# Moving the maxima and turns of Wk, Wv and Wo between the first batch's projections in an attention kernel on one Trainium2 core

## The reference

```python
def ref(x, adj, Wq, Wk, Wv, Wo):            # x: 32,256,512  adj: 32,256,256  W*: 512,512
    h = jnp.maximum(_layernorm(x, axis=-1), 0.0)
    q, k, v = (split_heads(h @ W.T) for W in (Wq, Wk, Wv))     # 16 heads of 32
    a = jnp.einsum('bhnd,bhmd->bhnm', q, k) * D ** (-0.5) + 2 * adj[:, None]
    row_nonzero = jnp.any(a != 0, axis=-1, keepdims=True)
    p = softmax(where(row_nonzero, a, -inf)); p = where(isnan(p), 0, p)
    o = jnp.einsum('bhnm,bhmd->bhnd', p, v)
    return x + merge_heads(o) @ Wo.T
```

## Time and profile before

| what | value |
|---|---|
| median of 3 runs | 1030.49 us (1030.35 to 1031.45) |
| profiled execution, its own time | 1030.06 us |
| its span, first to last instruction | 1028.3 us |
| mean granted PE clock | 0.983 of full speed |
| busy: PE, DVE, ACT, POOL | 980.3, 880.8, 930.1, 886.2 us |
| first exponentials on ACT | at 46.71 us |

### The profile page before, as it was taken

One profiled execution on the slowest core, in us unless ns is written; L12 is line 12 of the kernel. 1 busy time (PEld: TensorE's weight loads), 2 busy tenths in 40 slices (PEclk: granted clock), 3 DMA queues, 4 the chain that ended last, 5 costly groups with the idle time before them and its releaser, 6 DMA issues.

```text
span 1028.3 us, 34209 instructions
## 1 busy us (share of the span) xinstructions
PE 980.3 (95%) x11596; PEld 662.6 (64%) x11596; DVE 880.8 (86%) x3218; ACT 930.1 (90%) x3025; POOL 886.2 (86%) x1064
## 2 busy tenths in 40 slices
PE   6779999999999999999999999999999999999976
PEld 5556666666666666676666666666666666666733
DVE  6788998888899888899888889988888998888873
ACT  3499999999999999999999999999999999999992
POOL 1189998999999999999999999999999999999894
PEclk9899999999999999999999999999999999999978
DMA  6089999999999899999999999999999998999995
GB/s 245 11 144 173 190 185 170 191 181 187 187 188 194 174 187 175 190 186 189 188 176 185 182 186 183 192 172 189 179 186 190 187 196 173 187 175 167 164 173 128
DMA packets 569582, 182.62 MB, mean 178 GB/s; under 512 B 542784, under 2 KB 550976, under 8 KB 569408
## 3 DMA queue, kind: packets, MB, share of 16 engines
q1 hardware_dynamic: 569408, 180.43, 93.8%
HBM read 29.36 MB, written 16.78 MB: 45 GB/s over the span
## 4 chain that ended last, share of the span: by engine, by line
PE 40%; POOL 31%; ACT 19%; issue 6%; DVE 2%; DMA 1%; ACTq 0%; SPq 0%; POOLq 0%; DVEq 0%
PE ps L953 26%; POOL p L394 17%; ACT probs L488 13%; PE ps L1025 5%; PE ps L971 5%; POOL xn L374 4%; POOL o_lo L416 4%; ACT p L501 4%; POOL o_hi L413 2%; POOL rstd L368 2%; PE ps L836 2%; ACT v_hi L528 2%; POOL norm L403 2%; DVE w_max L589 1%; PE ps L999 1%
## 5 line engine op out<-in xcount | busy, mean ns | idle before, releaser
L394 POOL TENSOR_TENSOR p<-probs,p 128x512 f16<-128x512 f32 x512 | 588.7, 1160 | 86.9 <-ACT p L501 82.7
L488 ACT ACTIVATE probs<-logits,row_min 128x256 f32<-128x256 f32 x1024 | 508.7, 502 | 2.6 <-DVE row_min L669 2.6
L669 DVE CUSTOM_DVE_ANT_0 logits<-ps,adj_s,sigma 128x256 f32<-128x256 f32 x1024 | 441.3, 476 | 20.2 <-PE ps L971 13.2
L501 ACT ACTIVATE p<-probs 128x512 f16<-128x512 f32 x512 | 318.6, 622 | 0.0
L953 PE MATMUL ps<-ht_hi,w_hi 128*128 128x256 f16 x1024 | 279.7, 273 | 1.2 <-DVE q_lo L731 1.2
L953 PE MATMUL ps<-ht_hi,w_lo 128*128 128x256 f16 x1024 | 279.3, 273 | 0.0
L953 PE MATMUL ps<-ht_lo,w_hi 128*128 128x256 f16 x1024 | 279.3, 273 | 0.0
L488 ACT ACTIVATION_READ_ACCUMULATOR probs<-logits,row_min 128x1 f32 x1024 | 200.2, 196 | 0.0
L953 PEld LDWEIGHTS ps<-ht_hi,w_hi 128*128 128x128 f16 x1024 | 100.2, 98 | 21.7 <-issue 6.8
L953 PEld LDWEIGHTS ps<-ht_lo,w_hi 128*128 128x128 f16 x1024 | 100.3, 98 | 14.6
L953 PEld LDWEIGHTS ps<-ht_hi,w_lo 128*128 128x128 f16 x1024 | 100.3, 98 | 11.7
(11 more groups left out here) (84 smaller groups left out, 1659.1 us busy)
## 6 DMA issues: line engine op xcount, KB each, us to landing
xs<-in_x SPq DMA_DIRECT2D x32, 512.0 KB, 4.5
out<-xs SPq DMA_DIRECT2D x64, 256.0 KB, 2.6
adj_raw<-in_adj SPq DMA_DIRECT2D x32, 256.0 KB, 4.0
pt<-p SPq DMA_TRANSPOSE x512, 3.4
w_nat<-in_L_gnn_Wq SPq DMA_DIRECT2D x1, 1024.0 KB, 6.4
w_nat<-in_L_gnn_Wk SPq DMA_DIRECT2D x1, 1024.0 KB, 9.1
w_nat<-in_L_gnn_Wv SPq DMA_DIRECT2D x1, 1024.0 KB, 11.3
w_nat<-in_L_gnn_Wo SPq DMA_DIRECT2D x1, 1024.0 KB, 13.2
```

Source lines behind the costliest of these rows:

```text
L394: g.tensor_tensor(p16[:, c % 2, k, 1], probs[:, h % 4].rearrange("p u n -> p (u n)"), p16[:, c % 2, k, 0], ALU.subtract).then_inc(p_split, 1)
L488: e = a.activation(probs[:, h % 4, u, :], logits[:, h % 4, u, :], ACT.Exp, bias=row_min[:, t.par(d), u, h:h + 1], scale=-1.0, accum_out=ro ...
L501: a.activation(p16[:, c % 2, k, 0], probs[:, h % 4].rearrange("p u n -> p (u n)"), ACT.Copy)\
L669: v.tensor_tensor_reduce(out=logits[:, h % 4, u, :], in0=ps[:, S_BANK + h % HC, N * u:N * u + N], in1=adj_s[:, t.par(d), u, :], scale=sigm ...
```

## The change

The change adds no arithmetic and takes none away. It does four things in the first batch.

- Wk's whole chain leaves the prologue. Its maximum, row maximum, scale and low parts go to steps 0 to 3 on DVE, its high parts to step 3 on ACT; on PE `turn_max(1)` comes behind the 24 products of the first half of Q, `spread_max(1)` and `turn_weights(1)` behind the next 12.
- Wv's chain goes a step or so later: maximum still in step 4, row maximum 6 to 7, scale 7 to 8, and on PE the turn of the maximum 7 to 8 (so behind all of K's second half) and the rest from 8 to 9. Wo's maximum goes from step 4 to step 10 on DVE, its turn of the maximum from 10 to 11, its spread from 11 to 12.
- The first projection on each weight waits for the chunk that it multiplies with next, not for all four.
- POOL's wait for two scales moves from the slot's head to just before `adj_s`.

```diff
@@ pool @@
             def scale_adj(t):
                 pool.wait_ge(adj_in[t.par(1)], 16 * t.half(1) + 16)
+                if t.first:
+
+                    pool.wait_ge(scales_ready, 2)
...
             def slot(t):
-                if t.first:
-
-                    pool.wait_ge(scales_ready, 2)
@@ scalar @@
             take_h(first, 1, 1, 2)
-            take_weights(1)
...
-                    if t.first and s == 8:
-                        take_weights(2)
+                    if t.first and s in (3, 9):
+                        take_weights(1 + s // 9)
@@ vector @@
             take_h(first, 1, 0, 1)
-            weight_max(1)
-            weight_row_max(1)
             weight_rest(0)
             take_h(first, 1, 1, 2)
-            weight_scale(1)
-            weight_rest(1)
...
-                        if s in (3, 4):
-                            weight_max(s - 1)
-                        if s in (6, 10):
-                            weight_row_max(2 + s // 10)
-                        if s in (7, 11):
-                            weight_scale(2 + s // 11)
-                        if s == 8:
-                            weight_rest(2)
+                        if s in (0, 4, 10):
+                            weight_max({0: 1, 4: 2, 10: 3}[s])
+                        if s in (1, 7, 11):
+                            weight_row_max({1: 1, 7: 2, 11: 3}[s])
+                        if s in (2, 8, 12):
+                            weight_scale({2: 1, 8: 2, 12: 3}[s])
+                        if s in (3, 8):
+                            weight_rest({3: 1, 8: 2}[s])
@@ tensor @@
             turn_h(first, 1, 1)
-            turn_max(1)
-            spread_max(1)
-            turn_weights(1)
...
-                    if t.first and j in (0, 2, 6):
-
-                        pe.wait_ge(wt_taken, NC * (1 + {0: 0, 2: 1, 6: 2}[j]))
...
-                for o, l, r, start, stop in products[half * part:half * part + half]:
+                for i in range(half * part, half * part + half):
+                    o, l, r, start, stop = products[i]
+                    if t.first and j in (0, 2, 6) and i < 12 and i % 3 == 0:
+
+                        pe.wait_ge(wt_taken, NC * {0: 0, 2: 1, 6: 2}[j] + i // 3 + 1)
...
-                        if s in (7, 10):
-                            turn_max(2 + s // 10)
                         if s in (8, 11):
-                            spread_max(2 + s // 11)
-                        if s == 8:
+                            turn_max(2 + s // 11)
+                        if s in (9, 12):
+                            spread_max(2 + s // 12)
+                        if s == 9:
                             turn_weights(2)
...
                     project(t, s)
+                    if t.first and s == 1:
+                        turn_max(1)
+                    if t.first and s == 2:
+                        spread_max(1)
+                        turn_weights(1)
```

## The result

The changed kernel takes 1034.11 us, the median of 7 runs (1033.17 to 1035.79), against 1030.35 us of the kernel before beside it (7 runs, 1029.26 to 1031.45). The ratio is 1.0042, 95% interval 1.0031 to 1.0054. The prediction was 1034.0, range 1031.9 to 1036.0, slower. The profiled execution took 1034.11 us with a span of 1032.3, 4.0 more than before.

The account below looks back on a forecast made before the run. DVE's work and waits up to Wo's row maximum were taken to set the end. Waits of 6.45 us against 2.93 gave +3.5, end times +3.75, taken as +3.6: 1033.7 profiled, median 1034.0, range 1031.9 to 1036.0.

Parts of the forecast that it names:

- What bounds it: First batch: DVE's work and waits ahead of Wo's row maximum set the end; a shift there shifts everything behind it.
- that stretch at 1.8 us: Second slot's V products at the low clock, 71.8 to 74 us; without it some 1.8 us would be gone in either kernel.
- Q at 16.6: PE's first product of Q was to start at 16.6 us instead of 19.89, 3.3 us earlier.
- The waits of 2.5 and 1.2: DVE waits 2.5 us for PE's turn of Wk's maximum behind 24 products, 1.2 more for its spread behind 12.
- The fall of the clock: PE's granted clock was to be 0.50 from 17.3 to 20.7 us over Q, making 16 products slow.
- Forecast waits 0.65, 0.5, 0.8, 0.5: DVE's waits for Wv's turn (0.65), Wv's spread (0.5), ACT's first high part of Wv (0.8) and Wo's turn (0.5).
- The second `q_lo`: DVE's second low part of Q, behind Wv's maximum, was to come about 0.5 us later than 28.74.
- my two sums: DVE's delay up to Wo's row maximum: +3.5 us by summed waits, +3.75 by end times; +3.6 taken.
- C: Rival: the start of Q sets the first scores after all, 3.3 us earlier, 1027.2 us; chance 0.06.
- D: Rival: the shift is absorbed because later waits are fixed by something that doesn't shift, 1030.5 us; chance 0.07.
- B: Rival: same order effect, but PE's clock stays high over Q, 1032.3 us; chance 0.2.
- E: Rival: PE's clock stays low for longer, 1035.5 to 1036.3 us; chance 0.07.

Follow-up runs that it names:

- filler_before_scores: Kernel before plus 30 turns of Wq on PE, output unread, in the pause ahead of Wo's spread; 1027.64 us, ratio 0.9965.
- best: wo_behind_scores with Wv's turn and spread earlier, Wo's row maximum in step 13, its spread in 15, and 24 filler turns on PE; 1025.79 us, ratio 0.9954.
- turn_12_earlier: Changed kernel with PE's turn of Wk's maximum behind 12 products instead of 24, its spread behind 24 instead of 36; 1032.18 us, ratio 1.0027.
- clock_filler: Changed kernel plus 16 turns of Wq on PE, output unread, between the input's last turn and Q's first product; 1032.30 us, ratio 1.0027.
- wo_max_in_gap: Changed kernel with Wo's maximum on DVE directly behind Wk's, in the 2.47 us wait for PE; 1029.94 us, ratio 0.9999.
- late_only: Changed kernel with Wk's whole chain back in the prologue, only Wv's and Wo's parts at the later steps; 1030.37 us, ratio 1.0007.
- wo_behind_scores: Kernel before with all of Wo's chain moved behind the first scores (maximum in step 12); 1026.16 us, ratio 0.9972.
- chunk_waits_only: Kernel before with only the single-chunk waits and POOL's moved wait; 1030.02 us, ratio 0.9999.
- wk_only: Changed kernel with Wv's and Wo's chains at the steps of the kernel before, so only Wk's chain is moved; 1032.75 us, ratio 1.0033.

## Why the prediction was right

**What bounds it.** That DVE's work and waits up to Wo's row maximum set the start, and that this passes to the end nearly unchanged, held. In eleven of the thirteen kernels of the table it was 980.5 to 982.2 us from the first exponentials to the end of the span, while the exponentials' own start ranged from 43.33 to 50.99. In filler_before_scores and best it was 978.9 and 979.1. Both profiles are the fastest executions of their kernels, and in both the second slot's V products had the high pitch, 0.22, where the earlier trace rows has the low clock. But four other profiles had that as well, with 980.5 to 981.4 us, so what made the rest stays open. The prediction priced that stretch at 1.8 us; the seven profiles with it have 981.5 us on the mean behind the exponentials' start, the six without it 980.2.

**The start of Q and the first wait.** Q at 16.6 was forecast; taking off the inputs' 0.38, it was 16.69. The waits of 2.5 and 1.2 were 2.47 and 1.34. turn_12_earlier changed both by what stands ahead of the turn and the spread on PE, clock_filler changed the first by the pace of the products ahead of it, and wo_max_in_gap filled the first with other work.

**The fall of the clock.** It was forecast from the row of before that it would come over Q, and it came in this profile, 0.50 from about 18 to 21 (windows view, columns as in the earlier trace rows):

```profile
18.00:19.00 1.00, 1.00 (x7) 0.74 (x5) 1.00 (x1) 0.00 (x0) 0.00 (x0) 0.50 0.97 349
20.00:21.00 1.00, 1.00 (x7) 0.69 (x6) 0.00 (x0) 0.00 (x0) 0.00 (x0) 0.50 0.00 0
```

That it fell over Q in just this execution was partly luck: in two profiles of experiments it didn't. The Trainium skill ("TensorE: Matmul & The Clock Gate", "What's actually happening") says that the point of change varies between runs of one kernel. The traces agree: the six kernels with this gap and no filler are alike on PE up to Q, and Q's products were mostly at the low pitch in four of the profiles and at the high one in two.

**Wv and Wo.** Forecast waits 0.65, 0.5, 0.8, 0.5; measured 0.73, 0.53, 0.83, 0.47. The second `q_lo` came 0.83 later than before after the inputs' 0.38 is taken off (0.5 forecast), and Wo's row maximum 4.16 later (3.6).

**The sum.** This is where a size was off. The waits grew by 3.92 us, not 3.5, since four of the eight were 0.08 to 0.14 longer than I had them. The rest of the 4.16 is 0.24 that stands in no bracket. I had seen some 0.25 between my two sums and called it rounding, but the rows show a cost: an instruction of DVE that is followed at once gives way to the next before its own end (the `ht_lo` at 18.47 in the earlier trace rows is 0.67 long, and the next starts 0.60 after it), and one that stands in front of a wait doesn't (the `ht_lo` in front of the changed kernel's first 0.24 counts 0.69; the row maximum counts 0.28 there and 0.21 elsewhere). The changed kernel has eight waits where the kernel before has five, and three times 0.08 is 0.24, an estimate from these rows.

That the median came out within 0.1 of the forecast is in part luck. The profiled execution was forecast at 1033.7 and took 1034.11, 0.4 more. I had placed the median 0.3 above the forecast of the profiled execution, and there was no such distance: the profiled execution and the median are both 1034.11.

**Rivals.** C (Q's start sets the scores) and D (absorbed) fell by the profile. B and E were about the clock: B's high clock over Q was seen in two experiments' profiles, not in the changed kernel's, and the changed kernel's fastest execution took 1033.17, above B's 1032.3. E's long low stretch over Q was not seen.

**What stays open.** Three of my medians for experiments were 1.4 to 1.5 us too high (late_only, wo_max_in_gap, wo_behind_scores). 0.35 to 0.49 us of each is the kernel before's median, which was lower in those rounds, and by its ratio wo_behind_scores is no miss. I had built them on the one profile of the kernel before, in which the exponentials began 7.59 us after Wo's row maximum. In chunk_waits_only, which has the same order there, it was 6.65, and the low clock lasted from about 40.3 to 43.8 instead of 37.8 to 44.6. filler_before_scores shows that the low clock lengthens this distance; that its varying length explains all of the three misses is argued, not shown. The split of the changed kernel's loss between the order of PE's work and the clock over Q isn't shown in time either; it is read from the waits of single profiles.

## What to carry to other kernels

When a chain over engines (reduce, turn, reduce, spread, scale) is moved between long blocks of one engine's work, each hop waits for the block that it was put behind. Here DVE waited 3.8 us for two hops, for which it had waited 0.36 before the change, although Q started 2.8 us earlier. List the waits of the engine that sets the end, and ask of each moved step whether it fills one or makes one: the same 2.2 us reduction was free in one place and not in another. And what nothing needs until later, as Wo's scale, belongs behind the first critical result, not ahead of it.

## What the runs showed of the hardware that was not expected

A granted clock of 1.00 in a window doesn't always mean the high level. In wk_only PE's timeline has the low pitch from 16.8 to 19.6, and the windows view gives 1.00 for the same stretch:

```profile
17.01 0.42 PE L949 MATMUL ps<-ht_lo,w_hi 128*128 128x256 f16 x1
17.22 0.42 PE L949 MATMUL ps<-ht_hi,w_lo 128*128 128x256 f16 x1
```

```profile
17.00:18.00 1.00, 1.00 (x6) 0.74 (x5) 1.00 (x1) 0.00 (x0) 0.00 (x0) 1.00 1.08 369
```

The granted clock reads 1.00 from the start of that profile's span to 33 us. The pitch of 0.21 us is what like matmuls have at a granted clock of 0.50 (18 to 21 us in the changed kernel), against 0.11 at 1.00. Ahead of the first recorded change, the pitch of like matmuls is what to read.

Idle PE in the first batch can be worth filling with matmuls that nobody reads: 30 turns in a pause of 4 us took 0.35% off the kernel before (interval 0.22% to 0.47%). For the 16 turns in the gap of 2.4 us ahead of Q a gain is not shown.
